# Cross-attention on one core: the low halves of the folded products issued on half or a quarter of TensorE's array

## The reference

```python
qh = (q @ Wq + bq).reshape(Bn, Tq, H, DK)
kh = (k @ Wk + bk).reshape(Bn, Tk, H, DK)
vh = (v @ Wv + bv).reshape(Bn, Tk, H, DK)
attn = jnp.einsum('bqhd,bkhd->hbqk', qh, kh) * mask[None]
attn = attn - jnp.max(attn)
attn = jnp.exp(attn) * mask[None]
attn = attn / (jnp.sum(attn, axis=-1, keepdims=True) + 1e-15)
out = jnp.einsum('hbqk,bkhd->bqhd', attn, vh).reshape(Bn, Tq, H * DK) @ Wo + bo
x = out + residual
...   # layer norm of x, with gamma and beta
```

## Time and profile before

| what | value |
|---|---|
| median of 3 runs | 1735.91 us (1733.51 to 1736.13) |
| the profiled execution, its own time | 1737.56 us |
| its span | 1735.8 us |
| PE busy | 1676.3 us, 97% of the span |
| DVE, ACT, POOL busy | 66%, 54%, 24% |
| mean granted TensorE clock | 0.988 of full speed |
| DMA | 181 GB/s over the span |

### The profile page before, as it was taken

The page is one execution under the profiler, slowest core; times in us unless marked ns, Lnnn a source line. Parts: engine busy times, 40 slices in busy tenths (PEclk is TensorE's granted clock), DMA queues, the critical chain, the costliest instruction groups (busy, mean ns, idle before and its releaser), DMA issues. The chain is left out here.

```text
span 1735.8 us, 31156 instructions
## 1 busy us (share of the span) xinstructions
PE 1676.3 (97%) x11011; PEld 858.7 (49%) x11012; DVE 1153.6 (66%) x2346; ACT 938.8 (54%) x1413; POOL 419.0 (24%) x519
## 2 busy tenths in 40 slices
PE   4989999999999999999995999999999999999997
PEld 4545556455564655646542444444444444444443
DVE  7756555655556654565544877787787878787774
ACT  7745555455555555455544556555555656555542
POOL 0000000000000000000000455555555555555556
PEclk8999999999999999999996999999999999999999
DMA  6464344443544526445235356555654556555621
GB/s 231 146 230 141 146 182 163 178 167 121 205 159 161 187 91 235 137 168 196 74 146 209 139 230 242 217 206 205 242 209 186 194 233 242 217 201 210 242 104 67
DMA packets 81469, 315.01 MB, mean 181 GB/s; under 512 B 5392, under 2 KB 9616, under 8 KB 71696
## 3 DMA queue, kind: packets, MB, share of 16 engines
q1 hardware_dynamic: 81424, 314.41, 49.4%
HBM read 184.37 MB, written 130.02 MB: 181 GB/s over the span
## 5 line engine op out<-in xcount | busy, mean ns | idle before, releaser
L70 PE MATMUL ps_s<-x_hi,g_hi 128*128 128x512 f16 x1024 | 388.4, 379 | 7.0 <-ACT s L494 7.0
L79 PE MATMUL ps_o<-u,p_hi 128*128 128x512 f16 x1024 | 389.3, 380 | 0.0
L80 PE MATMUL ps_o<-u,p_hi 128*128 128x512 f16 x1024 | 388.9, 380 | 0.0
L81 PE MATMUL ps_o<-u,p_lo 128*128 128x512 f16 x1024 | 388.6, 380 | 0.0
L71 PE MATMUL ps_s<-x_lo,g_hi 128*128 128x512 f16 x1024 | 388.1, 379 | 0.0
L72 PE MATMUL ps_s<-x_hi,g_lo 128*128 128x512 f16 x1024 | 388.1, 379 | 0.0
L494 ACT ACTIVATE s<-ps_s,c_bias 128x512 f32<-128x512 f32 x256 | 175.8, 687 | 334.1 <-PE ps_s L72 330.2
L603 DVE TENSOR_TENSOR score_max<-score_max,tile_max 128x1 f32<-128x1 f32 x257 | 40.8, 159 | 339.2 <-ACT s L494 336.9
L870 ACT ACTIVATE p_hi<-ps_bc 128x512 f16<-128x512 f32 x256 | 149.4, 593 | 178.5 <-DVE ps_bc L960 176.6
L1051 POOL PARTITION_ALL_REDUCE key_max<-score_max x1 | 0.4, 377 | 922.8 <-issue 922.8
L1071 POOL TENSOR_TENSOR y<-y,gamma_b 128x512 f32<-128x512 f32 x128 | 162.7, 1271 | 192.7 <-ACT y L880 192.7
(11 more groups left out here) (85 smaller groups left out, 2423.0 us busy)
## 6 DMA issues: line engine op xcount, KB each, us to landing
scores<-s SPq DMA_DIRECT2D x30, 2048.0 KB, 7.6
s<-scores SPq DMA_DIRECT2D x30, 2048.0 KB, 7.7
x<-xT_in SPq DMA_DIRECT2D x32, 1024.0 KB, 9.7
u_halves<-u_out SPq DMA_DIRECT2D x64, 512.0 KB, 2.9
u<-u_halves SPq DMA_DIRECT2D x16, 2048.0 KB, 11.8
y<-x_in SPq DMA_DIRECT2D x32, 1024.0 KB, 10.0
out<-y SPq DMA_DIRECT2D x31, 1024.0 KB, 4.3
mask<-maskT_in SPq DMA_DIRECT2D x32, 256.0 KB, 10.3
```

Of the source, the lines that this page charges most:

```text
L70: pe.matmul(out, lhs_hi, rhs_hi, start=first, stop=False)
L79: pe.matmul(out, lhs_hi, rhs_hi, start=False, stop=False, skip_group_check=True)
L80: pe.matmul(out, lhs_hi, rhs_lo, start=False, stop=False, skip_group_check=True)
L81: return pe.matmul(out, lhs_lo, rhs_hi, start=False, stop=False, skip_group_check=True)
```

## The change

The zero rows of `kv_lo` are no longer multiplied. Each lo matmul of the folds contracts over 64 rows only:

- `fold_q`: the two tiles of a pair are now one head each (`of_half`, `folded`), all four chunks. For each chunk stand two hi matmuls on the full array, one into each tile, and then two lo matmuls from 64 rows and 128 columns, head 0 from rows 0 to 63, head 1 from rows 64 to 127. Both tiles are waited for and released together.
- `fold_o`: two tiles at a time, of pairs q and q+4: four hi matmuls as before (128 rows, 64 columns), then four lo matmuls of 64 rows by 64 columns, one in each quarter of the array. For pairs 4 to 7 the lo values and the hi weights therefore lie in the other head's rows (`rows_of_lo`), and `u2` is read at `place(p)`.
- `bias`: the lo product is two matmuls of 64 rows, 64 columns and one moving column each, in place of one.
- ACT rounds the last two weight chunks once more (the four parts of `wo2` for pairs 4 to 7, into the lo places), since the rows differ. DVE's `split_kv` for values is four instructions of half the size in place of two.

The diff, cut to its core:

```diff
+def rows_of_lo(p, h):
+    return 1 - h if p >= NP // 2 else h
...
-def fold_head_outputs(pe, bank, kv_hi, kv_lo, wo2, p, b):
-    for k, half in enumerate((kv_hi, kv_lo)):
-        for h in range(2):
-            mm = pe.matmul(bank[rows_of(h), :], half[:, p, b, h, :], wo2[:, p, h, :], ...)
+def fold_head_outputs(pe, banks, kv_hi, kv_lo, wo2, pairs, b):
+    for bank, p in zip(banks, pairs):
+        for h in range(2):
+            pe.matmul(bank[rows_of(h), :], kv_hi[:, p, b, h, :], wo2[:, p, h, :], ...)
+    for bank, p in zip(banks, pairs):
+        for h in range(2):
+            rows = rows_of(rows_of_lo(p, h))
+            mm = pe.matmul(bank[rows_of(h), :], kv_lo[rows, p, b, h, :], wo2[rows, p, h, :], ...)
...
             def bias(g, pairs):
-                        for k, half in enumerate((kv_hi, kv_lo)):
-                            mm = pe.matmul(o, half[:, p, b, :, :]..., bq2[:, p, :], ...)
+                        pe.matmul(o, kv_hi[:, p, b, :, :]..., bq2[:, p, :], ...)
+                        for h in range(2):
+                            mm = pe.matmul(o[rows_of(h), h:h + 1], kv_lo[rows_of(h), p, b, h, :],
+                                           bq2[rows_of(h), p, h:h + 1], ...)
...
             def fold_q(g, p):
-                for i in (2 * p, 2 * p + 1):
-                    pe.wait_ge(f_lo_done, g * FT + i + 1)
-                    for j in range(2):
-                        for h in range(2):
-                            for k, half in enumerate((kv_hi, kv_lo)):
-                                mm = pe.matmul(tile[:, j, :, h, :], wq2[:, p, h, cols], half[:, p, :, h, :], ...)
-                    mm.then_inc(f_summed, 1)
+                pe.wait_ge(f_lo_done, g * FT + 2 * p + 2)
+                for c in range(DC):
+                    for h in range(2):
+                        pe.matmul(tiles[h][:, c, :, :], wq2[:, p, h, cols], kv_hi[:, p, :, h, :], ...)
+                    for h in range(2):
+                        mm = pe.matmul(tiles[h][:, c, :, :], wq2[rows_of(h), p, h, cols], kv_lo[rows_of(h), p, :, h, :], ...)
+                mm.then_inc(f_summed, 2)
...
             def fold_o(g, q, first):
-                    pe.wait_ge(w_lo_done, 13 + q)
-                for j in range(QU):
+                    pe.wait_ge(w_lo_done, 15 + q // 2)
+                for j in range(0, QU, 2):
...
             def split_weight(i):                       # on ACT
                     rounded = act.activation(hi, w, ACT.Copy, scale=W_SCALE)
+                    if i >= 14:
+                        rounded = act.activation(lo, w, ACT.Copy, scale=W_SCALE)
```

More of the change, by code:

```diff
@@ L106, in projected, with place @@
     return kv32[rows_of(h), :, :].rearrange("r p (b k) -> r (p b) k", b=GB)
-def split_heads(dve, kv_lo, kv_hi, kv32, scale, done):
-    for h in range(2):
-        dve.scalar_tensor_tensor(of_head(kv_lo, h, h), projected(kv32, h), scale, of_head(kv_hi, h, h),
-                                 ALU.mult, ALU.subtract).then_inc(done, 1)
-def fold_head_outputs(pe, bank, kv_hi, kv_lo, wo2, p, b):
-    for k, half in enumerate((kv_hi, kv_lo)):
-        for h in range(2):
-            mm = pe.matmul(bank[rows_of(h), :], half[:, p, b, h, :], wo2[:, p, h, :],
-                           start=(k == 0), stop=(k == 1), skip_group_check=True)
+def rows_of_lo(p, h):
+    return 1 - h if p >= NP // 2 else h
+def place(p):
+    return 2 * (p % (NP // 2)) + p // (NP // 2)
+def fold_head_outputs(pe, banks, kv_hi, kv_lo, wo2, pairs, b):
+    for bank, p in zip(banks, pairs):
+        for h in range(2):
+            pe.matmul(bank[rows_of(h), :], kv_hi[:, p, b, h, :], wo2[:, p, h, :],
+                      start=True, stop=False, skip_group_check=True)
+    for bank, p in zip(banks, pairs):
+        for h in range(2):
+            rows = rows_of(rows_of_lo(p, h))
+            mm = pe.matmul(bank[rows_of(h), :], kv_lo[rows, p, b, h, :], wo2[rows, p, h, :],
+                           start=False, stop=True, skip_group_check=True)
     return mm
@@ L194, in weight_parts @@
                 for h in range(2):
-                    yield (*(w2[rows_of(rows), 2 * c:2 * c + 2, h, :] for rows in (h, 1 - h)),
+                    hi = h if i < 8 else rows_of_lo(2 * c, h)
+                    yield (*(w2[rows_of(rows), 2 * c:2 * c + 2, h, :] for rows in (hi, 1 - hi)),
                            w32_i[rows_of(h), :].rearrange("r (p d) -> r p d", p=2))
@@ L334, in bias @@
                         o = ps_k[0][:, 2 * (GB * p + b):2 * (GB * p + b) + 2]
-                        for k, half in enumerate((kv_hi, kv_lo)):
-                            mm = pe.matmul(o, half[:, p, b, :, :].rearrange("r h k -> r (h k)"), bq2[:, p, :],
-                                           start=(k == 0), stop=(k == 1))
+                        pe.matmul(o, kv_hi[:, p, b, :, :].rearrange("r h k -> r (h k)"), bq2[:, p, :],
+                                  start=True, stop=False, skip_group_check=True)
+                        for h in range(2):
+                            mm = pe.matmul(o[rows_of(h), h:h + 1], kv_lo[rows_of(h), p, b, h, :],
+                                           bq2[rows_of(h), p, h:h + 1], start=False, stop=True, skip_group_check=True)
                 if p == NP - 1:
@@ L345, in fold_q @@
                     pe.wait_ge(kv_lo_done, 4 * g + 2)
-                for i in (2 * p, 2 * p + 1):
-                    dp = i % 2
-                    pe.wait_ge(f_lo_done, g * FT + i + 1)
-                    tile = ps_f[i % GBANKS][:, :].rearrange("r (j b h k) -> r j b h k", j=2, b=GB, h=2)
-                    for j in range(2):
-                        cols = slice((2 * dp + j) * P, (2 * dp + j + 1) * P)
-                        for h in range(2):
-                            for k, half in enumerate((kv_hi, kv_lo)):
-                                mm = pe.matmul(tile[:, j, :, h, :], wq2[:, p, h, cols], half[:, p, :, h, :],
-                                               start=(k == 0), stop=(k == 1))
-                    mm.then_inc(f_summed, 1)
+                pe.wait_ge(f_lo_done, g * FT + 2 * p + 2)
+                tiles = [ps_f[(2 * p + h) % GBANKS][:, :].rearrange("r (c b k) -> r c b k", c=DC, b=GB) for h in range(2)]
+                for c in range(DC):
+                    cols = slice(c * P, (c + 1) * P)
+                    for h in range(2):
+                        pe.matmul(tiles[h][:, c, :, :], wq2[:, p, h, cols], kv_hi[:, p, :, h, :], start=True, stop=False)
+                    for h in range(2):
+                        mm = pe.matmul(tiles[h][:, c, :, :], wq2[rows_of(h), p, h, cols], kv_lo[rows_of(h), p, :, h, :],
+                                       start=False, stop=True)
+                mm.then_inc(f_summed, 2)
             def fold_o(g, q, first):
@@ L364, in fold_o @@
                 if first:
-                    pe.wait_ge(w_lo_done, 13 + q)
-                for j in range(QU):
+                    pe.wait_ge(w_lo_done, 15 + q // 2)
+                for j in range(0, QU, 2):
                     i, f = u_tile(g, q, j)
-                    pe.wait_ge(f_lo_done, i + 1)
-                    fold_head_outputs(pe, ps_f[f % GBANKS], kv_hi, kv_lo, wo2, 2 * q + j % 2, j // 2)\
-                        .then_inc(f_summed, 1)
+                    pe.wait_ge(f_lo_done, i + 2)
+                    banks = [ps_f[(f + k) % GBANKS] for k in range(2)]
+                    fold_head_outputs(pe, banks, kv_hi, kv_lo, wo2, (q, q + NP // 2), j // 2).then_inc(f_summed, 2)
             def scores(g, u, first):
@@ L456, in round_g @@
                 for i in (2 * p, 2 * p + 1):
[L457 removed]
                     act.wait_ge(f_summed, g * FT + i + 1)
[L459 to L460 removed]
+                    act.activation(of_half(g_hi, p, i % 2), folded(i), ACT.Copy, scale=G_SCALE / (W_SCALE * K_SCALE))\
                        .then_inc(f_hi_done, 1)
@@ L547, in split_weight @@
                 for hi, lo, w in weight_parts(i):
-                    split = dve.scalar_tensor_tensor(lo, w, W_SCALE, hi, ALU.mult, ALU.subtract)
+                    split = dve.scalar_tensor_tensor(lo, w, W_SCALE, hi if i < 14 else lo, ALU.mult, ALU.subtract)
                 split.then_inc(w_lo_done, 1)
@@ L559, in split_x, with split_kv @@
                                          ALU.mult, ALU.subtract).then_inc(x_lo_done, 1)
-            def split_kv(i, scale):
+            def split_kv(i, scale, values):
                 dve.wait_ge(kv_hi_done, 4 * i + 2)
-                split_heads(dve, kv_lo, kv_hi, kv32, scale, kv_lo_done)
+                for h in range(2):
+                    if not values:
+                        split = dve.scalar_tensor_tensor(of_head(kv_lo, h, h), projected(kv32, h), scale, of_head(kv_hi, h, h),
+                                                         ALU.mult, ALU.subtract)
+                    else:
+                        for k in range(2):
+                            pairs = slice(k * NP, (k + 1) * NP)
```

(17 more changed lines are left out.)

6 lines of the change are left out of this document (5 added, 1 removed).

## The result

The changed kernel takes 1823.71 us (median of 4 runs, 1822.05 to 1825.04) against 1736.02 us before (4 runs): a ratio of 1.0506, 95% interval [1.0488, 1.0525], 87.7 us slower. The forecast was 1800 us with a range to 1828. The direction and the price of a switch were right. The loss came out 24 us larger than forecast, mostly because PE's clock fell, which the forecast had left out.

A forecast was written before the change was run, and what follows sets the result against it. PE, busy 97% of the span, sets the time. Per group 6.1 + 2.0 - 0.4 = 7.7 us, eight groups 62 us, with ACT's 2 us 64 us more: forecast 1800 us, own range 1775 to 1828, stated range 1732 to 1828.

The forecast's parts named there:

- the price of a switch: PE's stall when the used array shape changes: 0.112 us each, from the quad's column changes, applied to row changes too.
- A: Rival, chance 0.11: switches between small matmuls on PE are nearly free, so saved steps count: 1720 us.
- B: Rival, chance 0.14: changing rows alone is free, changing columns is not, so only bias pays: 1732 us.
- C: Rival, chance 0.07: a switch costs half behind short matmuls, near 0.05 us: 1752 us.
- fold_q and bias: In the scores phase, a fold_q chunk goes from 0.22 to 0.39 us, a bias product from 0.05 to 0.255 us.
- PE alone counts: In the stage at a group's head, waits for DVE vanish and PE's steps set the time: 6.1 us more.
- the DVE comparison: In the stage, DVE's 1.2 us per pair hides under PE's 2.6 us, so waiting for two banks adds nothing.
- ACT's 2 us: Group 0: ACT rounding two weight chunks twice costs 2 us in all, between 0 and 4.
- E: Rival, chance 0.05: PE's clock falls in the stage, 64 us on top of the forecast, 1865 us.
- its own sign of being wrong: Listed sign that the forecast fails: PE's clock in a stage is below 1.00.
- 864 s - 27: Whole kernel's change in us at price s per switch, for 864 new switches; it turns faster below s = 0.031 us.
- Rival D: Chance 0.08: in fold_o's lo steps, halves writing one bank take turns, 14 us on top of the forecast, 1814 us.

The follow-up runs named there:

- q_full: Kernel before with the new fold_q order, tile layout and paired release, but lo matmuls on the whole array: 1745.6 us, ratio 1.0047 to before.
- bias_alone: Kernel before with only the bias of the changed kernel (lo product as two quarter-array matmuls): 1755.6 us, ratio 1.0101.
- q_alone: Kernel before with only the new fold_q, round_g and split_g, lo products on half arrays: 1797.6 us, ratio 1.0346.
- o_alone: Kernel before with only the new fold_o, a separate buffer for values' lo halves and ACT's second roundings: 1738.0 us, ratio 1.0009.
- o_grouped: o_alone with each quad's eight hi matmuls first and its eight lo ones behind them: 1729.7 us, ratio 0.9951 to before.

## Why the prediction was right, and where it was short

- *The price of a switch, from the quad's borders.* Right. It was the number taken from another kind of switch, and rows alone cost about what columns cost: (0.38 - 0.167) / 2 = 0.107 us in fold_q. Rivals A, B and C fall with it.
- *fold_q and bias.* 0.38 and 0.23 us at full clock, forecast 0.39 and 0.255. A group's cost at full clock is 5.3 us in the stage (5 x 1.52 + 16 x 0.23 = 11.3 against 5.96), 1.9 in the other folds, 0.3 less in the quads, so 6.9 to 7.0 us; forecast 7.7. Groups 2 to 7 of the kernel before have 5.96 and not group 1's 5.79, a small part of that difference.
- *"PE alone counts" in the stage.* Right as to waits: DVE's g_lo is waited for 0.5 us in all. (A third wait at the fold, once for kv_lo in group 0, was left out of the prediction's list: 6.7 us in the earlier trace rows, 7.6 in the changed kernel.) But the price of releasing two tiles together, which the prediction set at nothing under the DVE comparison, is 8 to 9 us once PE is quick (q_full). That the copies of G in 8 pieces cost nothing was right (ACT 594 ns against 595, DVE 686 against 684).
- *ACT's 2 us.* The wait grew from 1.94 to 3.94 us as forecast. That the clock then falls behind it for 3.4 us was not in it.
- *The clock.* Here the forecast was short. It had the clock at full speed and put the fall into a rival of its own (E, 0.05), as if it excluded the forecast, though it only adds to it. A clock below 1.00 in a stage was its own sign of being wrong, and it came true. Measured: 11.0 - 7.0 = 4.0 us a group in groups 1 to 7, 28 us; E's own price was 64. The argument against it, that the stretch is never idle, was not enough: in group 1 the clock fell with PE listed as busy throughout. The earlier trace rows could not tell this beforehand, since its window at 0.50 stands behind a long wait.
- *The sum.* 8 x 7.0 = 56, 7 x 4.0 = 28, and 4 us more in group 0 (133.75 us from its stage to the next instead of 122.67, less its 7.0) make 88 us; measured in the profiled executions 1824.85 - 1737.56 = 87.3. In group 0 these are ACT's wait and a clock that was at 1.2 GHz without a break until 47.5 us, 4 us into the scores, where in the kernel before it was back at 39.0, the stage's end.
- *The range.* That 1823.7 lies inside it is luck. It was made for the price of a switch and for ACT. With these as measured and the clock at full speed the sum is 56 + 2 = 58 us, 1794; the clock, which the range gives nothing, carried the time close to its upper end. And that end rests on a slip. The line 864 s - 27 does not come out of the prediction's own parts, which give 864 s - 33 with ACT's 2 us (at s = 0.112 that is the 64 us of the forecast, where 864 s - 27 is 70). By the parts the upper end would be 1822 and not 1828, just below what was measured.
- *Rival D.* Out: a lo step of four quarters takes one step and one switch, 0.34 us.

*The skill.* The Trainium skill, "TensorEngine Tiling (Array Packing)", section Tiling Modes, has a change of mode drain the engine. The traces here agree as far as they show it: a stall of 0.10 to 0.12 us stands at each of them, by rows, by columns and by both. The bank rule that rival D took from its Restrictions and Gotchas cost nothing here: a step of four lo matmuls took 0.34 us with its switch, and the two that write one bank from different row halves write different partitions.

*Open.* Why the low time is 10 us in some groups and nearly 14 in others (windows of groups 1 and 2), and why bias_alone's 8.15 us stage kept its clock while q_alone's fell: in bias_alone the folds run on the whole array step by step between the thin stretches, which fits, but no run separated this. What the clock follows is therefore not shown beyond this: it fell in the stretches broken by switches all along and not in the others, and less of it was lost where they were shorter.

## What to carry to other kernels

Count changes of the array's shape, not only matmuls: each cost 0.1 us, two steps of 128 columns or half a step of 512, so sort matmuls by shape and split only where the steps saved between two switches are worth more. A full busy share does not show it; the distance from start to start and the granted clock do. A stretch broken by switches all along can have a second price, the clock (here 28 of 88 us), and it adds to the first rather than being another outcome.

## What was not expected of the hardware

- PE's clock fell to 1.2 GHz in a stretch where PE was listed as busy without a break, 4.0 to 5.7 us after matmuls broken by switches began, and came back 1.7 to 4.3 us behind the stage's end.
- The clock was lost for 3.4 us behind a single wait of 3.9 us (changed kernel, o_alone), and for 6.8 around one of 3.27 us (o_alone). It was kept through waits of 3.51 us (kernel before) and 3.67 us (o_grouped), so the length of the wait alone does not decide it.
- Four quarter-array matmuls from two row halves, two of them into each of two banks, took the time of one, 0.34 us with its switch.
